# TensorE's order within one step of the layer 1 attention: scores moved from second place to behind the output products

## The reference, cut to what matters

```python
x = layer_norm(x, g_norm)
q = x @ Wq                                  # 128 -> 1024
k, v = split(context @ Wkv)                 # 96 -> 2 x 1024
k = concat([null_k, k]); v = concat([null_v, v])
sim = einsum('bhid,bhjd->bhij', q, k) / 8   # 128 x 129 for a head
attn = softmax(sim)
out = einsum('bhij,bhjd->bhid', attn, v)    # 128 x 64 for a head
out = layer_norm(concat_heads(out) @ Wout, g_out)
```

## Time and profile before

| | us |
|---|---|
| median of 3 runs | 401.96 (400.99, 401.96, 410.23) |
| the profiled execution, its own time | 399.93 |
| its span, first to last instruction | 397.8 |

### The profile page before, as it was taken

How to read it: one execution, slowest core, us unless ns; L and a number is a source line. 1 busy time by engine, 2 the same in 40 slices (tenths; PEclk the granted TensorE clock), 3 DMA queues, 4 the chain that set the end, 5 groups by cost and what they waited for, 6 DMA issues and landing times.

```text
span 397.8 us, 8307 instructions
## 1 busy us (share of the span) xinstructions
PE 332.8 (84%) x2509; PEld 244.6 (61%) x2516; DVE 262.8 (66%) x764; ACT 241.7 (61%) x838; POOL 146.3 (37%) x248
## 2 busy tenths in 40 slices
PE   1899898899898577999999999999999998345422
PEld 1486485585485465777777777878778776222122
DVE  2758467547767645565967778585867868449774
ACT  1636956837756636767677677676776764138360
POOL 3132143142242124535636455463654536100022
PEclk9969999969999889999999999999999999758555
DMA  8920000000000100000000000000000000000002
GB/s 201 229 49 0 21 2 2 20 0 0 0 0 0 54 0 1 2 2 3 0 2 2 2 2 1 2 2 2 1 2 2 2 3 0 2 0 0 0 26 79
DMA packets 12466, 7.13 MB, mean 18 GB/s; under 512 B 3792, under 2 KB 11984, under 8 KB 12432
## 3 DMA queue, kind: packets, MB, share of 16 engines
q1 hardware_dynamic: 11712, 6.51, 6.4%
q10 hardware_dynamic: 720, 0.20, 0.2%
HBM read 5.66 MB, written 1.05 MB: 17 GB/s over the span
## 4 chain that ended last, share of the span: by engine, by line
PE 61%; DVE 17%; issue 7%; ACT 5%; POOL 4%; DMA 2%; SPq 1%; DVEq 1%; ACTq 0%; POOLq 0%
PE psum L854 13%; PE psum L962 9%; PE psum L1148 9%; PE psum L858 7%; PE psum L1162 7%; PE psum L860 3%; PE psum L859 3%; DVE work L1360 2%; POOL rstd L486 2%; PE psum L992 2%; DMA KT<-in_L_xattn_Wkv 2%; DVE st L1351 2%; PE psum L1049 1%; PE psum L1179 1%; DVE work L1643 1%
## 5 line engine op out<-in xcount | busy, mean ns | idle before, releaser
L800 ACT ACTIVATE work<-psum,nmx 128x129 f32<-128x129 f32 x256 | 84.7, 389 | 10.5 <-DVE nmx L1507 10.5
L854 PE MATMUL psum<-ident,work 128*128 128x128 f32 (+2 forms) x416 | 69.1, 293 | 17.5 <-DVE work L1625 4.9
L1501 DVE COPY work<-psum 128x512 f32<-128x512 f32 x64 | 43.9, 685 | 47.7 <-PE psum L854 47.5
L854 PEld LDWEIGHTS psum<-ident,work 128*128 128x128 f32 (+2 forms) x416 | 46.4, 146 | 37.3 <-issue 15.1
L566 POOL TENSOR_TENSOR work<-work,rden 128x512 f32<-128x512 f32 x64 | 67.6, 1056 | 0.0
L858 PE MATMUL psum<-split 128*128 128x256 f32 (+2 forms) x128 | 56.9, 445 | 0.1
L800 ACT ACTIVATION_READ_ACCUMULATOR work<-psum,nmx 128x1 f32 x256 | 50.9, 199 | 0.0
L962 PE MATMUL psum<-KT,work 64*128 64x129 f32 x512 | 45.8, 297 | 2.0 <-DVE den L1517 1.3
L791 ACT ACTIVATE work<-psum 128x256 f32<-128x256 f32 x56 | 21.5, 384 | 42.7 <-PE psum L860 42.7
L1507 DVE TENSOR_REDUCE nmx<-psum 128x4 f32<-128x516 f32 x64 | 44.3, 692 | 3.4 <-PE psum L962 3.4
L860 PE MATMUL psum<-split 128*128 128x256 f32 (+2 forms) x128 | 44.5, 348 | 0.0
(11 more groups left out here) (173 smaller groups left out, 532.7 us busy)
## 6 DMA issues: line engine op xcount, KB each, us to landing
out_x<-X SPq DMA_DIRECT2D x4, 256.0 KB, 2.3
KT<-in_L_xattn_Wkv SPq DMA_DIRECT2D x2, 384.0 KB, 6.0
X<-in_x SPq DMA_DIRECT2D x1, 768.0 KB, 7.6
work<-in_ctx SPq DMA_DIRECT2D x3, 192.0 KB, 2.5
work<-in_L_xattn_Wq SPq DMA_DIRECT2D x1, 512.0 KB, 8.2
KT<-in_L_xattn_Wout SPq DMA_DIRECT2D x1, 512.0 KB, 5.5
work<-in_L_xattn_Wout SPq DMA_DIRECT2D x1, 512.0 KB, 3.9
X<-in_x SPq DMA_DIRECT2D x1, 256.0 KB, 2.8
```

Source lines behind the costliest of these rows:

```text
L800: ins = act.activation(Sx[n % 4][:, j, :], psum[:, here, (j // 2) * K1:(j // 2 + 1) * K1], ACT.Exp, bias=nmx[n % 2][:, j:j + 1], accum_out ...
L854: return pe.transpose(dst, src, ident[0:m, 0:m])
L1501: dve.tensor_copy(PTs[m % 2], bank[4]).then_inc(pt_out.sem, 1)
```

## The change

In TensorE's iteration, `scores(n)` moves from behind the transposes to behind the query chunk, the output products and the two null steps, right ahead of `values(n - 3)`. No other line changes, and the streams of the other engines stay as they are.

```diff
             for n in range(LAST + 1):
                 if live(n - T_LAG):
                     p_transposes(n - T_LAG)
-                if live(n) and n > 0:
-                    scores(n)
                 if q_chunk(n):
                     t, c = q_chunk(n)
                     pe.wait_ge(xs_ready.sem, xs_ready.at(t + 1))
@@
                 t = pair_at(n, PNT_AT)
                 if t is not None:
                     null_transposes(t)
+                if live(n) and n > 0:
+                    scores(n)
                 if live(n - T_LAG):
                     t = pair_at(n, NULL_AT)
                     if t is not None:
                         pe.wait_ge(pnt_out.sem, pnt_out.at(t + 1))
                     values(n - T_LAG)
```

## The result

The changed kernel takes 469.93 us (median of 4 runs, 466.62 to 471.58) against 401.94: ratio 1.170, interval 1.164 to 1.175. The profiled execution took 466.62 us with a span of 464.4. The forecast was 467, range 454 to 482. Some executions of one and the same kernel take over 1.5% longer than its fastest; the ratios and intervals here leave them out, the medians do not.

What follows compares the result with a forecast made beforehand. The prediction took TensorE as the bound before, and after the change a closed round of 3.88 us an iteration. The profiled 399.93 + 67.4 for the attention + 0.4 for iteration 3 gave 467.7, say 467 us, range 454 to 482.

Steps and rivals of the forecast that it cites:

- What bounds the kernel before: In the attention before the change, TensorE is the bound, busy 165.84 of 168 us, at 2.82 us a step.
- the 1.12 us between copy and output products: Before the change, ScalarE's copy starts 1.12 us ahead of the output products that use it, so the chain costs nothing.
- the prediction's own fourth link: From the start of ScalarE's copy to the start of TensorE's output products: 0.52 us.
- The closed round: In the new order, scores, maxima, exponentials, copy and output products close on themselves once in every iteration, 60 rounds.
- Its length, 3.88 us: Round of five links: scores-maxima 0.76, maxima-exponentials 0.73, exponentials-copy 1.23, copy-products 0.52, products to next group 0.64; 2.82 before.
- The sum over the attention, 241.0 us: 60 rounds of 3.88, 232.8 us, plus null_out 4.5, null transposes 1.5 and y_evac 2.2; 241.0 against 173.6.
- rival 2: TensorE's clock falls to half as it idles; steps of 4.8 us bound by its stream, 528 us in all; 4%.
- The wait of the output products, 0.96 us: TensorE's output products wait 0.96 us for ScalarE's copy in each iteration, 50 to 60 us in the waits.
- The saved change of shape: On TensorE, one array-shape change fewer an iteration saves 0.20 us, 12 us in all, lying in the wait, not forecast.
- Rival 1: TensorE's streams bound the kernel and shape changes are saved: 388 us with one saved, 376 with two; 4%.
- Rival 3: The attention's round is shorter than the links' sum, halfway at 3.35 us, giving 436 us; 5%.
- Rival 4: VectorE's norms delay maxima in three iterations of eight, 1.31 not 0.76 after scores: 12 us more, 479; 86% with forecast.

Runs made afterwards that it cites:

- e5: Kernel before the change, with three tiny exponentials added on ScalarE behind exponents(n) in each iteration: 405.4 us, ratio 1.005.
- e1: Changed kernel, with ScalarE's copy for the output products moved ahead of exponents(n), for unit n - 3: 418.1 us, ratio 1.040.
- e8: e1 with ScalarE's other two copies, y_evac and pn_evac, also one iteration earlier, ahead of the exponentials: 401.1 us, ratio 0.995.
- e6: Changed kernel, with TensorE's output products one iteration later, out_proj(n - 5) instead of out_proj(n - 4): 410.5 us, ratio 1.021.
- e3: Changed kernel, with the scores moved only half the way, behind the query chunk but ahead of the output products: 405.8 us, ratio 1.005.
- e9: e8 with values and output products one iteration later, values(n - 4) and out_proj(n - 5): 396.6 us, ratio 0.987.
- e12: e9 run once more, unchanged, beside e10: 396.6 us, ratio 0.989.
- e10: e9 with TensorE's old order, scores behind the transposes, same lags and early copies: 401.6 us, ratio 0.999.
- e4: Changed kernel, with three tiny exponentials added on ScalarE behind exponents(n) in each iteration: 486.9 us, ratio 1.205.

## Why the prediction was right, step by step

- **What bounds the kernel before, and the 1.12 us between copy and output products.** Shown by e5: from unit 5 on, a dose of 0.28 us on ScalarE costs 0.9 us where it costs 14.8 in the changed order. But 1.12 us is not the slack, as I took it in e5's expectation: the output products can't start until 0.52 us after the copy, by the prediction's own fourth link, so the slack in the step shown is 0.60. In two of the plain iterations of each pair the distance is 0.78, the slack 0.26, a little less than the dose. This changes no term of the sum.
- **The closed round.** Shown three ways: opened on ScalarE (e1, e8), opened on TensorE (e6), and avoided by passing only query chunk and not output products (e3), the loss goes from 17.0% to 4.0 and -0.5% (e1, e8), 2.1% (e6) and 0.5% (e3).
- **Its length, 3.88 us.** Plain rounds measure 3.88. All five links, taken from the trace before, held within 0.01 us. They summed because none of them had slack in it where it was read. In the three links from one engine to another the later engine was waiting: VectorE 2.74 us for the scores, ScalarE 0.62 us for the maxima, and for the copy TensorE's weight load, in a line that stands right ahead of the matmuls of the earlier trace rows:

```profile
318.36 0.52 PEld L1162 LDWEIGHTS psum<-work 128*128 128x128 f32 x4 [0.22 <-ACT work L774]
```

  The other two, exponentials to copy and output products to the next group, are one engine's own work in a row.
- **Output products to scores 0.64 and not 0.54.** 232.43 to 233.07 is 0.64.
- **The sum over the attention, 241.0 us.** 241.5. The `y_evac` iterations take 4.15, 0.27 more than plain ones (0.31 forecast), those with the null transposes 4.10 (0.22 more, as forecast), those with `null_out` 4.51 (0.63 more, 0.64 forecast). From the scores of unit 1 to those of unit 3 it is 4.37 us against 4.02: 0.35, 0.4 forecast. The end's -0.8 is inside the 2 us of gain that the range had. That the total comes within 0.5 us is in part luck: 1.0 of the 241.5 is the low clock of rival 2, which the sum did not have, so without it the sum is some 0.5 too high.
- **The wait of the output products, 0.96 us.** 60.5 us in 59 waits, 1.03 each (50 to 60 us forecast). The stream between scores and output products is a little shorter than the 2.28 I added up, as the query chunk no longer changes the array's shape; the round hides it.
- **The saved change of shape is not in the sum.** Right for this kernel. In e1 and e9, where TensorE's stream is the bound, it is there: 2.62 against 2.82 us.
- **Rival 1** (the streams bound it) has fallen: it needs the round under 2.28 us. Its price of 12 us fits what was seen: e9 and e12 against e10 show 5 to 6 of it, and 5.4 are found in the iterations that VectorE makes late.
- **Rival 2** (the clock). It did come, for some 7 us: from 387.1 to 394.0 us the granted clock is 0.50, the lower level of 1.2 GHz. The query chunks had ended with iteration 57, and in the round just ahead of the fall TensorE waited 1.61 of 4.15 us. The two rounds that the stay touches take 4.39 us each.

```profile
390.39 1.23 PE L962 MATMUL psum<-KT,work 64*128 64x129 f32 x8
...
391.56 1.12 PE L1148 MATMUL psum<-work,V 128*64 128x128 f32 x8
...
392.61 1.12 PE L854 MATMUL psum<-ident,work 128*128 128x128 f32 x4
...
394.14 0.71 PE L1162 MATMUL psum<-work 128*128 128x128 f32 x4 [0.42 <-ACT work L774]
```

  I had said that the clock stays at 1.00 to the attention's end; it didn't. Each of the two rounds was slow in one part only: the first in its output products (1.15 us to the next scores, 389.24 to 390.39, for 0.64), the second in its scores (maxima 1.28 after them for 0.76). A round wholly at the lower clock would have both, 3.88 + 0.51 + 0.52 = 4.91 us by the chain, an estimate. These rounds also have no query chunk. Where e4's clock fell in the middle of the attention, with a query chunk, the output products waited only 0.18 us, though the dose made the chain longer:

```profile
204.60 0.56 PE L861 MATMUL psum<-split 128*128 128x256 f32 x1
...
205.77 1.07 PE L1165 MATMUL psum<-work 128*128 128x128 f32 x4 [0.18 <-ACT work L775]
```

  With groups at the lower clock read from start to start (scores 1.17, values 1.05 and output products 1.15 in the changed kernel; transposes 0.77, 203.83 to 204.60, and a query chunk 0.92, 162.60 to 163.52, in e4), TensorE's stream takes 5.06 us. So a step of about 5 us, bound by the stream, is the estimate from these rows, and my price of 4.8 us was near it, a little low; no run here has a whole attention at the lower clock. From 150 to 380 us, with TensorE busy 75% and transposes among its work, the clock is 1.00.
- **Rival 3** (the round is shorter than the sum) has fallen: rounds of 3.88 us, not 3.35; no link started early.
- **Rival 4** (norms hold up the maxima). As expected it vanished: maxima start 0.76 us after the scores in all rounds but one, the second of the two at the lower clock. Its price was too high as well: before, the three late iterations of a pair were at 1.19, 1.21 and, in some pairs only, 1.31 us, not all at 1.31.

Did scores to values count as a change of shape? The last six scores and the first two values, in narrow windows of the changed kernel:

```profile
217.50 0.50 PE L962 MATMUL psum<-KT,work 64*128 64x129 f32 x6
...
217.94 0.33 PE L1148 MATMUL psum<-work,V 128*64 128x128 f32 x2
```

The last scores start at 217.50 + 0.50 - 0.27 = 217.73, the values 0.21 later by these rounded rows: the gap that stands at a change of shape, 0.20 from transposes to scores. Half arrays of rows and half arrays of columns side by side save one change in four, not two. By the rule of the Trainium skill (TensorEngine Tiling (Array Packing), Key Properties: changing the mode, not just the tile, drains the engine) it should be so, and the trace agrees, by the gap of 0.21 us.

What stays open: the median is 3.3 us above the profiled execution, and only one execution is profiled. Between the profiled executions of different kernels, differences of that size lie ahead of the attention; whether they do between the executions of this kernel was not seen.

## What to carry to other kernels

Before a group of instructions is moved in an in-order stream, write down for each wait in that stream which work the waited-for result itself needs, through the other engines' own orders; if the moved group is in that list and now stands behind the wait, the chain becomes a round once per iteration. Where its latency is longer than the stream, that latency is the new period, however little the engines have to do. Here such a round could be summed beforehand to a hundredth of a us, because each link from one engine to the next was read at a place where the later engine was waiting. A distance read where nobody waits, like the 1.12 us from copy to output products, still has a latency in it (0.52) and is not slack. A gain inside the stream (here 0.20 us an iteration) is only there after the slack has been put back, by placing the copies ahead of the long work and giving each result one iteration more.

## What was not expected

A change of array shape from 64 rows to 64 columns costs as much as one between the full array and 64 rows: 0.20 us from start to start, where transposes follow each other at 0.11. Three exponentials of one column cost 0.28 us together: they start 0.09 us apart, though all three are recorded as 0.44 us from the first's start to the last's end. And with identical code ahead of it, the attention starts up to 9 us apart from one profiled run to another, more than the effect of most edits here: a stretch inside the profile tells apart what the whole time can't, as long as the granted clock is the same in it.
